# Turned ring places, and parts of the next batch's first tiles among the last token tiles of an attention and int8 feed-forward kernel

## The reference

```python
q = (X @ Wq).reshape(b, t, NH, HD).transpose(0, 2, 1, 3)      # NH = 16, HD = 64
k = (X @ Wk).reshape(b, t, NKV, HD).transpose(0, 2, 1, 3)     # NKV = 8
v = (X @ Wv).reshape(b, t, NKV, HD).transpose(0, 2, 1, 3)
q = q * cos + _rotate_half(q) * sin
k = k * cos + _rotate_half(k) * sin
k = jnp.repeat(k, n_rep, axis=1)
v = jnp.repeat(v, n_rep, axis=1)
att = jnp.einsum('bhqd,bhkd->bhqk', q, k) * 256.0 ** (-0.5)
att = SOFTCAP * jnp.tanh(att / SOFTCAP)                       # SOFTCAP = 50
att = jnp.where(causal[None, None], att, -jnp.inf)
att = jax.nn.softmax(att, axis=-1)
y = jnp.einsum('bhqk,bhkd->bhqd', att, v)
x = _layernorm(x + y.transpose(0, 2, 1, 3).reshape(b, t, NH * HD) @ Wo)

absmax = jnp.max(jnp.abs(x), axis=-1, keepdims=True)
scale = jnp.maximum(absmax, eps) / 127.0
q8 = jnp.clip(jnp.round(x / scale), -128, 127).astype(jnp.int8)
acc = jnp.einsum('bsk,nk->bsn', q8, weight, preferred_element_type=jnp.int32)
x = _layernorm(x + (acc * scale * w_scale[:, 0] + bias).astype(jnp.float16))
```

## Time and profile before

| | |
|---|---|
| time, median of three | 1494.65 us |
| profiled execution, its own time | 1498.59 us |
| span of its instructions | 1496.8 us |
| mean granted clock of PE | 0.939 |
| busy: PE, DVE, ACT, POOL | 1327.0 us (89%), 1094.6 (73%), 847.4 (57%), 379.1 (25%) |
| chain that ended last | PE 55%, SP's queue 14%, DVE 11%, DMA 7%, issue 6%, ACT 3%, POOL 3% |
| DMA | 196.23 MB, mean 131 GB/s |
| transfers for sums | 256 of 64 KB, 128 of 2 KB |
| transfers that put keys and queries | 256 of 128 KB, 512 of 64 KB |

### The profile page before, as it was taken

How to read it: one execution, slowest core, us unless ns; L and a number is a source line. 1 busy time by engine, 2 the same in 40 slices (tenths; PEclk the granted TensorE clock), 3 DMA queues, 4 the chain that set the end, 5 groups by cost and what they waited for, 6 DMA issues and landing times.

```text
span 1496.8 us, 17694 instructions
## 1 busy us (share of the span) xinstructions
PE 1327.0 (89%) x5824; PEld 964.5 (64%) x5840; DVE 1094.6 (73%) x1367; ACT 847.4 (57%) x952; POOL 379.1 (25%) x448
## 2 busy tenths in 40 slices
PE   6479999888987999998987999989799799999794
PEld 5356777666665777675755677767576577776462
DVE  4368888782687788885477788878357788888485
ACT  4156777761236777864232877676223486779332
POOL 2231111111462111110265112111136311111275
PEclk9889999998998999999899899999899899999896
DMA  7755445474424345537341444445642244343431
GB/s 281 259 194 153 114 112 133 115 213 158 129 61 105 92 115 133 165 84 222 127 140 50 109 118 124 107 146 149 207 136 79 79 115 107 99 108 105 152 108 42
DMA packets 117038, 196.23 MB, mean 131 GB/s; under 512 B 28498, under 2 KB 70484, under 8 KB 112724
## 3 DMA queue, kind: packets, MB, share of 16 engines
q1 hardware_dynamic: 112340, 186.73, 44.1%
q10 hardware_dynamic: 4608, 8.39, 1.5%
HBM read 89.39 MB, written 38.54 MB: 85 GB/s over the span
## 4 chain that ended last, share of the span: by engine, by line
PE 55%; SPq 14%; DVE 11%; DMA 7%; issue 6%; ACT 3%; POOL 3%; DVEq 0%; ACTq 0%; POOLq 0%
PE ps L720 18%; PE ps L694 13%; PE ps L643 13%; SPq L474 8%; PE ps L757 6%; PE ps L665 4%; SPq L487 3%; DMA d_scratch<-sums 2%; DMA rows<-r_scratch 2%; SPq L465 1%; DMA qk<-work_r 1%; ACT probs L888 1%; DVE probs L1138 1%; DVE stats L1159 1%; SPq L490 1%
## 5 line engine op out<-in xcount | busy, mean ns | idle before, releaser
L720 PE MATMUL ps<-prob_hi,v 128*65 128x512 f32 (+3 forms) x1280 | 415.0, 374 | 5.9 <-DVE prob_lo L1077 5.9
L694 PE MATMUL ps<-qk 128*128 128x512 f32 (+1 forms) x1280 | 326.8, 382 | 71.7 <-DMA qk<-work_r 40.3
L888 ACT ACTIVATE probs<-ps 128x1024 f32<-128x1024 f32 x288 | 293.4, 1019 | 148.6 <-PE ps L694 147.2
L1077 DVE TENSOR_TENSOR prob_lo<-probs,prob_hi 128x1024 fp32r<-128x1024 f32 x288 | 355.6, 1235 | 9.9
L1286 POOL TENSOR_SCALAR_AFFINE_SELECT probs<-probs 128x256 f32<-128x256 f32 (+1 forms) x192 | 144.7, 761 | 805.4 <-ACT probs L893 805.4
L694 PEld LDWEIGHTS ps<-qk 128*128 128x128 f32 x1280 | 230.4, 194 | 137.6 <-issue 39.7
L893 ACT ACTIVATE probs<-probs 128x1024 f32<-128x1024 f32 x288 | 305.7, 1061 | 8.8
L1073 DVE CAST prob_hi<-probs 128x1024 fp32r<-128x1024 f32 x288 | 205.9, 715 | 128.4 <-POOL probs L1286 80.1
L643 PE MATMUL ps<-xT,w_ring 128*128 128x512 f32 x1152 | 291.2, 398 | 1.6 <-DVE v L1022 1.5
L643 PEld LDWEIGHTS ps<-xT,w_ring 128*128 128x128 f32 x1152 | 218.9, 192 | 48.5 <-issue 2.2
L720 PE MATMUL ps<-prob_lo,v 128*65 128x512 f32 (+1 forms) x640 | 238.8, 373 | 0.0
(11 more groups left out here) (77 smaller groups left out, 1041.7 us busy)
## 6 DMA issues: line engine op xcount, KB each, us to landing
qk<-work_r SPq DMA_DIRECT2D x256, 128.0 KB, 2.3
qk<-work_r SPq DMA_DIRECT2D x512, 64.0 KB, 2.0
y_scratch<-sums SPq DMA_DIRECT2D x256, 64.0 KB
wo<-wo_scratch SPq DMA_DIRECT2D x8, 2048.0 KB, 8.0
y_raw<-y_scratch SPq DMA_DIRECT2D x32, 512.0 KB, 3.6
w_ring<-w_scratch SPq DMA_DIRECT2D x15, 1024.0 KB, 5.3
x_raw<-X_T SPq DMA_DIRECT2D x16, 512.0 KB, 5.8
x_in<-X SPq DMA_DIRECT2D x32, 256.0 KB, 2.8
```

Of the source, the lines that this page charges most:

```text
L694: mm = nc.tensor.matmul(scores[:, g % 2, col:col + REP * w].rearrange("p (h q) -> p h q", h=REP), qk[:, n % 2, i, 2 + part, keys], qk[:, n ...
L720: mm = nc.tensor.matmul(sums_ps[:, :, GQ - w:GQ], v[:, kt, v0:v0 + width], p[:, g % ring, col:col + REP * w].rearrange("p (h q) -> p h q", ...
L888: nc.scalar.activation(probs[:, g % PRING, :], scores[:, g % 2, :], ACT.Tanh, scale=SCORE_SCALE / SOFTCAP).then_inc(capped, 1)
L1077: nc.vector.tensor_tensor(prob_lo[:, g % PRING, :], probs[:, g % PRING, :], prob_hi[:, g % HRING, :].bitcast(F32), ALU.subtract).then_inc( ...
```

## The change

- *Ring places.* Tile `g` lies in place (g + 3) % 4 of `probs` and `prob_lo` and (g + 2) % 3 of `prob_hi`. The waits of `cap` and `round_probs` on the last token tiles change with it: tile 0 waits for token tile 6's output projection, and its high part for token tile 7's.
- *First tiles.* For batches 1 to 3, score tiles 0 and 1 are made, capped, masked and split among the last two token tiles: PE `score(b + 1, 0)` after `linear` of token tile 6 and `score(b + 1, 1)` after that of 7; ACT caps tile 0 before `keep_q` of token 7 and tile 1 before `norm2` of token 7; POOL masks before `residual2` of token 6; DVE splits tile 0 after `rescale` of token 6 and tile 1 after that of 7. The loops skip these two steps.
- *Key chunk.* Of the second unit's chunks only the key chunk is projected there, in three parts of 8 in PROJ_BANK; the first query chunk goes to steps 5 to 7 of the first unit. DVE's rotation of the key chunk goes to step 3, the second chunk's to step 8, and all puts to the usual steps.
- *Sums.* `y_scratch` holds 65 rows, so values and divisors go out in one transfer of 65 partitions of 2 KB. `d_scratch` is gone. A y tile is loaded with two transfers of 64 partitions instead of one of 128.
- *Loads in pieces.* In unit 2 two token pieces are loaded in step 12, the third in step 14, the fourth and the query weights in step 15. The value weights are loaded in four parts, two in step 13 of the last unit, one each in 14 and 15.
- *Last unit.* The low half of its last put is issued by ACT after its last exponent. `invert(b, 0)` goes before the split of tile 70 in every batch. In the last batch the first spread goes before the last weighing and to another bank.
- *Key weights* for the third unit of a batch are loaded in step 3 of its first unit instead of behind the token tiles.

The diff, cut to its core:

```diff
-    y_scratch = nc.dram_tensor("y_scratch", [NT, P, KO, P], F32, kind="Internal").ap()
-    d_scratch = nc.dram_tensor("d_scratch", [NT, REP, KO, P], F32, kind="Internal").ap()
-    r_scratch = nc.dram_tensor("r_scratch", [2, NT, REP, KO, P], F32, kind="Internal").ap()
...
+    y_scratch = nc.dram_tensor("y_scratch", [G, VJ, KO, REP * GQ], F32, kind="Internal").ap()
+    r_scratch = nc.dram_tensor("r_scratch", [2, G, KO * REP * GQ], F32, kind="Internal").ap()
...
+        def prob_place(g):
+            return (g + 3) % PRING
+
+        def hi_place(g):
+            return (g + 2) % HRING
...
-            return m == 0 or (m % UB == 1 and m > 1 and x < 2)
+            return m == 0
...
+        def spread_bank(b, t):
+
+            return PROJ_BANK if (b, t) == (B - 1, 0) else SPREAD_BANK
...
+        def at_end(b, u, s):
+
+
+            return b >= 1 and u == 0 and s < 2
...
+        def put(eng, m, x, low):
+            eng.wait_ge(rope_lo if low else rope_hi, chunks_upto(m, x))
...
-                sp.dma_start(y_raw[:, y_place(t), :, :], y_scratch[t]).then_inc(y_loaded[t % YRING], 16)
+                for h in range(REP):
+                    n0 = h * GQ + t % 2 * P
+                    sp.dma_start(y_raw[h * HD:(h + 1) * HD, y_place(t), :, :], y_scratch[t // 2, 0:HD, :, n0:n0 + P]
...
-                sp.dma_start(div[:, c, :], d_scratch[2 * c:2 * c + 2].rearrange("t h j (a n) -> (t h j a) n", n=P // G)
...
+                sp.dma_start(div[:, c, :], y_scratch[c, ONE].rearrange("j n -> (j n)").rearrange("(p n) -> p n", p=P)
...
+                    sp.dma_start(r_scratch[part, c].rearrange("(p n) -> p n", p=P),
...
+                    sp.dma_start(rows[REP * part:REP * (part + 1), :].rearrange("h (k n) -> h k n", k=KO).bitcast(F32),
+                                 r_scratch[part, t // 2].rearrange("(k h t n) -> t h k n", k=KO, h=REP, t=2)[t % 2]
+                                 ).then_inc(rows_loaded, 16)
...
+                sp.dma_start(w_v[:, :, :, :].rearrange("p w k n -> p (w k n)")[:, cols].bitcast(F32),
+                             wv_scratch[:, cols]).then_inc(wv_loaded, 16)
...
-                for h in range(REP):
-                    sp.dma_start(y_scratch[2 * c:2 * c + 2, h * HD:(h + 1) * HD, j, :].rearrange("t d n -> d t n"),
-                                 sums[0:HD, slot, h * GQ:(h + 1) * GQ].rearrange("d (t n) -> d t n", t=2)
-                                 ).then_inc(sums_put[slot], 16)
-                sp.dma_start(d_scratch[2 * c:2 * c + 2, :, j, :].rearrange("t h n -> h t n").unsqueeze(0),
-                             sums[HD:HD + 1, slot, :].rearrange("a (h t n) -> a h t n", h=REP, t=2)
-                             ).then_inc(sums_put[slot], 16)
+                sp.dma_start(y_scratch[c, :, j, :], sums[0:VJ, slot, :]).then_inc(sums_put[slot], 16)
...
-                        if b >= 1 and u == 0 and s in (1, 2, 3, 4):
-                            put(m, *((0, 0), (1, 0), (0, 1), (1, 1))[s - 1])
...
+                        if s == 3 and m % UB and m + 1 < U:
+                            sp.wait_ge(projected, chunks_upto(m, 0))
+                            load_wk(m + 1)
...
+                            put(sp, *at, 0)
+                        if (at := chunk_at(b, u, s, turns(u, 6, 11, 15))) and at != (UB * b + UB, 2):
+                            put(sp, *at, 1)
...
                             sp.wait_ge(projected, chunks_upto(m, 2))
...
+                                load_x_turned(b + 1, 0)
+                                load_x_turned(b + 1, 1)
+                            elif m % UB == 0:
+                                load_wv(b + 1, 0)
+                                load_wv(b + 1, 1)
                             elif m + 1 < U:
                                 load_wq(m + 1)
+                        if u == 2 and b + 1 < B and s in (14, 15):
+                            load_x_turned(b + 1, s - 12)
+                            if s == 15:
+                                load_wq(m + 1)
+                        if u == UB - 1 and m < U and s in (14, 15):
+                            load_wv(b + 1, s - 12)
...
-                        score(b, g)
+                        if not at_end(b, u, s):
+                            score(b, g)
                         for part in range(3):
-                            if at := chunk_at(b, u, s - part, turns(u, 0, 5, 9)):
+                            at = chunk_at(b, u, s - part, turns(u, 0, 5, 9))
+                            if at and not (b >= 1 and u == 0 and at[1] == 0):
                                 project(*at, 8 * part, 8 * part + 8)
...
+                if not more:
+                    spread_rows(b, 0)
                 weigh(b, NB - 1)
-                spread_rows(b, 0)
+                if more:
+                    spread_rows(b, 0)
...
-                if more:
-                    project(m, 0, 0, 12)
                 turn_q(b, NT - 2)
                 if more:
-                    project(m, 0, 12, 24)
+                    project(m, 0, 0, 8)
                 linear(b, NT - 2)
                 if more:
-                    project(m, 1, 0, 12)
+                    score(b + 1, 0)
+                    project(m, 0, 8, 16)
                 turn_q(b, NT - 1)
                 if more:
-                    project(m, 1, 12, 24)
+                    project(m, 0, 16, 24)
                 linear(b, NT - 1)
+                if more:
+                    score(b + 1, 1)
...
-                    if g == PRING - 1:
-                        act.wait_ge(o_done, rows_upto(b - 1, NT - 1))
-                    for t in {1: (NT - 2, NT - 3), 2: (NT - 1,)}.get(g, ()):
+                    if g == 0:
+                        act.wait_ge(o_done, rows_upto(b - 1, NT - 2))
+                    for t in {2: (NT - 2, NT - 3), 3: (NT - 1,)}.get(g, ()):
                         act.wait_ge(out_stored[t % FRING], stores_upto(b - 1, t))
...
+                nc.scalar.activation(probs[:, prob_place(g), :], scores[:, g % 2, :], ACT.Tanh,
...
+                else:
+                    act.wait_ge(pv_done, scores_upto(b, NB - 4 + t))
...
-                        if b >= 1 and u == 0 and s in (1, 2):
-                            round_rope(UB * b + 1, s - 1)
...
+                        if at_end(b, u, s):
+                            continue
...
+                if more:
+                    put(act, UB * b + UB, 2, 1)
...
+                if more:
+                    cap(b + 1, 0)
+                    exponent(b + 1, 0)
                 keep_q(b, NT - 1)
                 norm2(b, NT - 2)
                 store(b, NT - 2)
+                if more:
+                    cap(b + 1, 1)
+                    exponent(b + 1, 1)
                 norm2(b, NT - 1)
                 store(b, NT - 1)
...
+                elif b >= 1:
+                    dve.wait_ge((o_done, acc_done, x2_done)[g], rows_upto(b - 1, NT - 1))
+                nc.vector.tensor_copy(prob_hi[:, hi_place(g), :], probs[:, prob_place(g), :]).then_inc(rounded, 1)
...
-                        if not more and u == UB - 1 and s == 17:
+                        if u == UB - 1 and s == 17:
                             invert(b, 0)
-                        if g >= 1:
+                        if g >= 1 and not at_end(b, u, s - 1):
                             probs_of(b, g - 1)
...
                 probs_of(b, NB - 1)
-                if more:
-                    invert(b, 0)
                 invert(b, 1)
...
                 if more:
-                    rope_read(m, 0)
+                    probs_of(b + 1, 0)
                 stats2(b, NT - 2)
                 shift_by(b, NT - 2, 1, rstd2, shift2)
                 rescale(b, NT - 1)
                 if more:
-                    rope_read(m, 1)
+                    probs_of(b + 1, 1)
                 stats2(b, NT - 1)
...
+                if b + 1 < B:
+                    mask(b + 1, 0)
                 residual2(b, NT - 2)
                 inverse_std(b, NT - 2, 1, mv2, veps2, rstd2, normed)
+                if b + 1 < B:
+                    mask(b + 1, 1)
                 residual2(b, NT - 1)
                 inverse_std(b, NT - 1, 1, mv2, veps2, rstd2, normed)
```

142 lines of the change are left out of this document (60 added, 82 removed).

## The result

The changed kernel takes 1503.4 us (median of 4, 1501.3 to 1504.7); the kernel before, on the same chip, 1495.8 (4 runs, 1493.5 to 1497.1). The ratio is 1.0046, with a 95% interval of 1.0027 to 1.0064: slower by 4 to 10 us. Forecast were 1476 us, with a range of 1456 to 1493. The profiled execution took 1501.25 us, span 1499.3, against 1498.59 and 1496.8 before.

The account below looks back on a forecast made before the run. PE, busy 89% of the span, was taken as the bound, with SP's queue suspected where it stands still. Terms -3.7 - 16 - 6 + 7 = -18.7 us from the median 1494.65 gave 1476 us, range 1456 to 1493.

Parts of the forecast that it names:

- A: Groups of sums on SP's queue: one transfer saves 1.4 us per group and removes the first-batch stall; minus 3.7 us.
- B: Start of each batch's last unit: put issued 5 to 6 us earlier, all four put waits go; minus 16 us.
- C: End of a batch: ACT's puts let SP start y loads 1.2 to 1.7 us earlier, so rows come earlier; minus 6 us.
- D: Three batch boundaries: score tiles and key chunk among the last tokens cost net 2.3 us each; plus 7 us.
- the 2.5 us taken: Batch boundary, after PE restarts at score tile 4: clock low for some 5 us, 2.5 us lost.
- the 3.3 taken: Batch boundary: POOL's residual beside DVE's split, taken as 3.3 us, between 2.5 alone and 4.5 one after the other.
- the Trainium skill's rule cited in the prediction: DVE and POOL share ports, so split and residual run one after the other: 4.5 us, sum 3.6 us higher.
- the signs of being wrong that the prediction named: Put waits stay, ACT's issues pass a microsecond, or last key chunk and tiles leave PE no idle time at the boundary.
- Rival 3: End of batch: ACT's puts slower, eight taking 14 us instead of 5, y loads later; 1508 us, chance 0.13.

Follow-up runs that it names:

- experiment 1: Kernel before with only the one transfer per group of sums and the layouts and loads that go with it: 1489.3 us, ratio 0.9927.
- the first try: Kernel after combining experiment 2, experiment 3, experiment 4 and experiment 6, query weights behind puts, a chunk one tile earlier, both Wo halves on ACT's queue: 1505.2 us, ratio 1.0051.
- experiment 3: Kernel after with the four token loads and the query weights issued in one go again: 1497.1 us, ratio 0.9995.
- experiment 4: Kernel after with all four quarters of the value weights loaded together at step 13: 1497.9 us, ratio 0.9990.
- experiment 6: Kernel after with SP's end-of-batch order changed, divisors, inverse sums and rows ahead of y loads, Wo's second half on ACT's queue: 1483.8 us, ratio 0.9914.
- experiment 5: Kernel after with the low half of the last put issued by SP again, not by ACT: 1508.8 us, ratio 1.0079.
- (7): Kernel after with each y tile loaded by one transfer of 128 partitions instead of two of 64: 1725.6 us, ratio 1.153.
- experiment 2: Kernel after without the two score tiles and the key chunk among the last tokens: 1501.1 us, ratio 1.0020.
- (11): Kernel of experiment 6 plus the edits of experiment 3 and experiment 4, score tiles and key chunk among the last tokens kept: 1460.9 us, ratio 0.9755.

## Why the prediction was wrong

**A, the one transfer (-3.7, and -4.8 in the profile): right.** The issue is 0.41 us (median; 0.30 to 1.55), where 0.5 was taken, the stall at 144.64 is gone, and the first unit gained 4.8, all of it between cap 4 (+0.1) and cap 18. What the prediction didn't ask is how much of B was A's: with A alone the waits of B fall from 11.4 to 7.1 us and the units gain 8.9, as much as with all of B (experiment 1). Alone it gained 11 us in time.

**B, the start of the last unit (-16, and -8.8 in the profile): a step that failed, by 7 us.** Its first half was right. The low put is issued 5.8 us earlier against the caps, as said (5 to 6), the four waits for puts are gone, and the premise that DVE has its data ready holds, with little to spare: the low part is done at 257.04, the put starts at 257.85. What failed is "PE is three tiles behind in the weighing and meets it only as one late tile, at most 1.4 us, of which I count 0.7 in three batches". PE meets the last token piece directly. The chunk that PE projects at the start of the last unit is the next batch's first, and `project` waits for all four token pieces; the last was issued behind the whole low put. DVE, SP's queue and ACT in the kernel after:

```profile
255.82 1.22 DVE L1097 TENSOR_TENSOR work_r<-work,work_r 128x1024 fp32r<-128x1024 f32 x1
```

```profile
257.85 4.95 SPq L427 DMA_DIRECT2D qk<-work_r  x8
262.84 0.59 SPq L436 DMA_DIRECT2D x_raw<-X_T  x1
```

```profile
266.39 1.06 ACT L864 ACTIVATE xT<-x_raw 128x1024 fp32r<-128x1024 f32 x1 [2.30 <-DMA x_raw<-X_T]
```

So one wait at the start of a unit took the place of another: 3.16, 3.14 and 1.69 us for the tokens in the first three batches, 8.0 in sum where the prediction counted 2.1, and where the puts had 2.92, 2.55 and 4.22. That 5.9 is most of the 7 us; the clock makes the rest. Six profiles with the pieces in this order have -0.7 to -8.8 in the units (mean -4.7), the kernel after being the lucky one; the five with the tokens at once and the one transfer, leaving out the first try, have -8.9 to -13.5 (mean -11.5). Without the pieces the waits for puts don't all go: 2.11, 1.40 and 2.14 us are left in experiment 3, 1.88, 2.18 and 3.06 in experiment 1. They are shorter than those for the tokens, and were less often followed by a low clock. So the pieces brought some 7 us in. The first eight products of that chunk read only the first half of the tokens, so a wait for two pieces would do for them; no run tried it.

**C, the end of a batch (-6, and +9.6 in the profile): the step that failed most, by 15.6 us.** ACT's puts came as said (eight in 5.17 us from 323.27) and were worth 5 us by the ratios, 3.3 by the table. Three terms were wrong. First, the y loads took more than was allowed:

```profile
331.94 2.62 SPq L448 DMA_DIRECT2D y_raw<-y_scratch  x4
...
350.26 0.56 SPq L471 DMA_DIRECT2D rows<-r_scratch  x2
```

0.80 became 2.62, 1.8 more, where 0.8 to 1.6 were taken, and they start only 0.5 us earlier against the caps (8.66 of the difference of 9.13 was there already), where 1.2 to 1.7 were expected: from the end of ACT's issues to the y loads it is 3.5 us, not 1.5 to 2. So the rows of tile 1 came later, not earlier: 353.52 is 2.2 us later than 359.96 by the same measure. Second, the last quarter of the value weights:

```profile
324.97 0.58 SPq L495 DMA_DIRECT2D w_v<-wv_scratch  x1
```

It was issued behind the eight transfers as predicted, but landed 5.8 us later, at 330.81, where 4 were taken; in the time of the profile before that is 339.5, not 336. PE stood 9.21 us for it instead of 5.87, and "It doesn't matter much, because the next thing PE needs, the rows, is set by SP" was half true: experiment 4 got back 8 us. It was also in the way of ACT's puts. Behind cap 71 the y loads start at 9.9, 10.5 and 10.1 us in the kernel after, no earlier than with all puts on SP and the weights in one go (9.9, 10.6, 9.9 in experiment 1), and at 7.8, 8.9 and 10.0 where ACT puts and the quarter is gone (experiment 4). Third, the premise that the rows are ruled by SP's work was true but read too narrowly. It was their place in the queue, behind y loads, 2 MB of Wo and a load of divisors that waits for sums, and experiment 6 changed that for 20 us.

By the table the ends come apart like this: +6.9 is there with the one transfer and its layouts alone (experiment 1), ACT's puts take 3.3 off (against experiment 5), and the weights in pieces add 4.9 (against experiment 4), 8.5 of the 9.6. That the 6.9 are the y loads in halves fits SP's queue, where against cap 71 the rows of tile 0 are issued 2.0 us later and those of tile 1 1.4 us later in the first batch of experiment 1; the experiment that was to single them out (7) met something else, so it isn't shown by a run.

**D, the boundary (+7): right, and by its own mechanism.** It is +7.6 by the profile; by the timed ratios 4 (experiment 2) and 6 (11), each with overlapping intervals. Tile 2 was capped at 460.26, 467.4 in the time of the profile before, against 465.9 to 467.0 predicted, and PE started tile 4 at 461.34, that is 468.5 against 467.0. From cap 0 to cap 2 it is 18.1 us, where the sum was 17.4. The clock behind it was a little kinder than the 2.5 us taken: 0.76 from 461.3 to 468.3, an estimate of 1.7 lost. DVE's split and POOL's residual met:

```profile
445.45 1.28 POOL L1341 TENSOR_TENSOR f<-probs,bias 128x512 f16<-128x512 f32 x1
446.81 1.50 POOL L1343 TENSOR_TENSOR probs<-f,z 128x512 f32<-128x512 f16 x1
```

```profile
445.52 1.76 DVE L1109 CAST prob_hi<-probs 128x1024 fp32r<-128x1024 f32 x1 [3.65 <-POOL probs L1317]
447.32 2.08 DVE L1113 TENSOR_TENSOR prob_lo<-probs,prob_hi 128x1024 fp32r<-128x1024 f32 x1
```

Alone the cast takes 0.69 and the subtraction 1.23, beside POOL 1.76 and 2.08. From 445.45 to 449.40 the two pieces of work took 3.95 us, between the 3.3 taken and the 4.5 of one after the other. The four instructions end one after another, at 446.73, 447.28, 448.31 and 449.40, each of the last three 0.14 us sooner than its time alone (0.69, 1.17, 1.23) would have it. That is nearly what the Trainium skill's rule cited in the prediction says, "SBUF — State Buffer", section "Who interferes with whom", less a little overlap, and it would have been the better estimate.

**The sum.** -3.7 - 16 - 6 + 7 became -4.8 - 8.8 + 9.6 + 7.6, which is +3.6 for the two profiled executions. The timed medians differ by 7.6, 4 more. The clock behind the new waits is a likely reason: the other five profiles with the pieces in this order have a mean of -3.8 in the units, 5 us above the kernel after's -8.8. It isn't shown, since the mean granted clocks of the timed runs (0.935 to 0.940) don't differ from the profiled one's 0.936. Of the signs of being wrong that the prediction named none came: they look for failures of its own terms, and what failed were terms that it had at little or nothing. None of the rivals had the mechanism. Rival 3 had the sign and the place, SP's chain from the y loads on at three boundaries, but laid it on ACT, whose issues took about as long as SP's.

## What to carry to other kernels

A transfer cut in pieces is as late as its last piece: before moving that piece behind other issues, look for the instruction that waits for all of them, and for which batch it is. A queue worked in order has to be read as a schedule: what stands in front of the transfer that the busiest engine asks for next, and does it have to? Here the order of a dozen transfers, with one moved to another queue, was worth 20 us, more than any one of the edits. And run each edit of a bundle by itself: one of the four was a gain of 0.7% that the others hid.

## What was not expected of the hardware

- A transfer whose access pattern has 2 as its outermost dimension ran on two of sixteen DMA engines (share 0.12 to 0.14, 36 to 44 GB/s) and held SP's queue for up to 11.9 us an issue.
- The same wait of PE, 3.16 and 3.34 us at the same place, was followed by a granted clock of 1.00 in one execution and 0.57 in another (the 6.9 us behind it). Of eighteen waits for the last token piece in six profiles (1.7 to 3.6 us), sixteen were followed by 0.56 to 0.77 and two by 1.00, both in the profile that was read first. One profile of a stage is a poor measure of what such a wait costs.
- A transfer of 64 KB (a put) landed 2.0 us behind its issue in the median of the kernel after, and 9.2 to 10.5 beside 4 MB on ACT's queue, whichever queue issued it; of two transfers of 16 KB issued 0.4 us apart, the one ahead of 2 MB on the other queue landed in 1.4 us and the one behind it in 7.4. In these runs a second queue saved issue time, not the sharing.
